# A four-layer graph network: norm, projections, split and logits of three graph stages, and one graph tail, each as one pipeline over node tiles

## The chip, the cores and the metric

The kernel runs on one core of a Trainium2 chip. The metric is the device time of one execution in microseconds; before the change it was 7021.22 us in the median of three runs (7018.96 to 7030.24). A core has a matmul engine (PE, with its weight loads as PEld), VectorE (DVE), ScalarE (ACT), GpSimd (POOL) and SyncE (SP), each with its own queue, and 16 DMA engines. They meet only through semaphores.

## The reference, cut to what matters

3125 nodes with 256 features, 53,125 edges. Each of four layers adds a graph stage, a mixing stage and a feed-forward stage to `x`. The change lies in the graph stages of layers 1 to 3.

```
xn = _layernorm(x)
# layer 1, graph stage
enh = xn + 0.1 * query_emb
Q, K, V = enh @ Wq + bq, enh @ Wk + bk, enh @ Wv + bv     # 4 heads of 64
scores  = sum(Q[dst] * (K[src] + 0.2 * rel)) / 8
agg     = segment_sum(softmax over dst(scores) * V[src], dst)
msgs    = where(deg > 0, agg, V)
y       = msgs @ Wo + bo + xn
g1      = (y - mean(y)) / sqrt(var(y) + 1e-5) * gamma + beta
x       = x + g1 + mix1(xn)
# layer 2: h = xn @ W + b; h_src = sum(h * a_src), h_trg = sum(h * a_trg), 8 heads of 32
# layer 3: support = xn @ weight; relu(segment_sum(support[src] * edge_weight, dst))
```

## The kernel before

The nodes are 25 tiles (`NT`) of 125 rows (`P`). `core.x`, `core.xn` hold them by rows, `core.xnT` by columns (the transposes of the normed rows). The program is a sequence of phases (`Phase`, line 81); each is a block with one program per engine, and closes with a barrier of all engines (line 97) that the trace names as `PEq L97` or `POOLq L97`. Within a phase the order on each engine is the order written, and waits are on semaphores. Nothing is scheduled by a planner.

Before each of the graph stages of layers 1 to 3 stands `layer_norm` (line 502): 25 statistics (line 546), thirteen small instructions over all tiles (552 to 565), then five tiles at a time the normed rows (595), two transposes a tile (651), the copy to `xnT` (637) and in layers 1 and 3 the copy to `xn` (614). `project` (line 655) loads its weights, multiplies 25 tiles (714) and adds the bias on the way out of PSUM (740, 745) or copies (757); with a `table` it writes five tiles per DMA through a ring of two slots (695).

Layer 1 (`gnn1`, line 3457): norm; `g1_enh` adds the query embedding to `xnT`; `project` for the queries; `split_rows` (2835) cuts them into three bf16 parts, in turns of ScalarE and VectorE; `project` for keys and values into the table `keyval1`; then `edge_scores` gathers rows of that table (3169). After scores and softmax `weighted_sums` (3373) reads weighted rows (`kept`) back, scales them on GpSimd (3414), sums them by node on the matmul engine (3425) and adds them up on VectorE (3439) in 440 steps. The tail: `g1_fin` reads all values back (3504) and chooses between sum and own value (3515 to 3521) in whole-tensor instructions, `transpose_rows` (2798), `project` with `Wo`, `add_rows` (3537), and `layer_norm` with gamma, beta and the addition to `x` (573 to 582).

Layer 2 (`gnn2_mix2`, line 3775): norm, `project`, then `g2_logit` with the two logit sums over all tiles (3809, 3810) and the table write (3799, 3802), and the addition of another bias to `x`. Then comes `linear_attention`, whose weights are loaded at lines 967 to 973. Layer 3 (`gnn3_mix3`, line 2570): norm, `project` into the table `support`, then the mixing stage, which gathers from it (837).

## Time and profile before

| | |
|---|---|
| median of three runs | 7021.22 us (7018.96 to 7030.24) |
| the profiled execution's own time | 7018.5 us |
| its span | 7016.7 us |
| mean granted matmul clock | 0.758 of full |
| PE busy | 4600.0 us (66%) |
| DVE busy | 3445.3 us (49%) |
| POOL busy | 2631.8 us (38%) |
| ACT busy | 1006.0 us (14%) |
| DMA | 616.64 MB, mean 88 GB/s |

The shares are means over stages with different limits: no engine is busy throughout, and the stretches that the change touches are read one by one below. Times in the rows are microseconds from the span's start unless marked ns.

### The profile page before, as it was taken

What the parts mean: (1) busy time and instruction counts of PE and PEld (TensorE: products, weight loads), DVE (VectorE), ACT (ScalarE), POOL (GpSimd) and SP (SyncE); (2) the same over time, 40 slices, a digit from 0 to 9 for tenths busy, and PEclk for the clock granted to TensorE, in tenths of its full rate; (3) what the DMA queues carried; (4) which work ended last, traced back from release to release, by engine and by line L of the source; (5) the groups of instructions that cost most, each with busy time, mean ns of one, the idle gap of its engine ahead of it and who ended that gap; (6) DMA issues with size and microseconds to landing.
All of it is one profiled execution on the core that took longest, in us unless ns stands there. A gap on an engine that the chain in (4) does not pass through costs nothing. (4 is left out here: it accounts for less than half of the span.)

```text
span 7016.7 us, 71368 instructions
## 1 busy us (share of the span) xinstructions
PE 4600.0 (66%) x17936; PEld 3173.8 (45%) x17936; DVE 3445.3 (49%) x8060; ACT 1006.0 (14%) x2236; POOL 2631.8 (38%) x2698
## 2 busy tenths in 40 slices
PE   0486755556784577748736646588759986767644
PEld 0244543334572343324335533476637764545443
DVE  6224444443004567769851255577742233566722
ACT  0121100002221000001112210000023331111111
POOL 2345556661100455537512200566500004555332
PEclk9877776667896575559858877656679998888767
DMA  4100013333111788856512210344410003222223
GB/s 141 46 2 2 2 40 92 92 92 82 37 39 43 224 254 255 249 166 197 153 64 82 78 36 0 100 114 114 94 38 0 0 0 104 71 73 72 68 91 108
DMA packets 407468, 616.64 MB, mean 88 GB/s; under 512 B 76191, under 2 KB 303918, under 8 KB 406741
## 3 DMA queue, kind: packets, MB, share of 16 engines
q0 software_dynamic: 124448, 324.61, 16.9%
q1 hardware_dynamic: 279540, 284.98, 12.9%
q10 hardware_dynamic: 3154, 3.20, 0.2%
q8 instruction: 144, 2.36, 0.1%
q14 instruction: 182, 1.48, 0.1%
HBM read 475.70 MB, written 137.50 MB: 87 GB/s over the span
## 5 line engine op out<-in xcount | busy, mean ns | idle before, releaser
L837 POOL DMA_INDIRECT m_rows<-support,far_at x440 | 421.7, 958 | 1133.1 <-POOLq L97 775.5
L3169 POOL DMA_INDIRECT g_sc_rows<-keyval,src_at x440 | 438.6, 997 | 520.0 <-DVE g1b_scores L3239 227.6
L3576 POOL DMA_INDIRECT g_sp_rows<-h,src_at x440 | 438.0, 996 | 464.6 <-POOLq L97 254.1
L493 POOL DMA_INDIRECT records<-record,place_at x416 | 416.2, 1001 | 408.5 <-issue 114.4
L847 PE MATMUL g_sums_bank<-g_sums_rows,g_sums_same 128*125 128x256 f32 x880 | 351.0, 536 | 292.6 <-issue 279.2
L837 POOL DMA_INDIRECT g_sums_rows<-h,far_at x440 | 416.0, 945 | 230.1 <-issue 111.1
L3624 PE MATMUL g_sp_bank<-g_sp_rows,g_sp_same 128*125 128x264 f32 x880 | 456.7, 618 | 46.0 <-issue 22.7
L3188 PE MATMUL g_sc_pair<-g1q_parts,g_sc_near 125*128 x1320 | 333.0, 384 | 170.8 <-DVE g_sc_rows L3235 112.0
L847 PEld LDWEIGHTS g_sums_bank<-g_sums_rows,g_sums_same 128*125 128x125 f32 x880 | 197.8, 255 | 445.7 <-issue 397.7
L847 PE MATMUL m_half<-m_rows,m_same 128*125 128x256 f32 x880 | 292.3, 436 | 130.5 <-issue 125.6
L879 DVE TENSOR_TENSOR g_total<-g_total,g_sums_bank 125x256 f32 x440 | 182.8, 415 | 332.9 <-issue 158.5
L879 DVE TENSOR_TENSOR g_total<-g_total,m_half 125x256 f32 x440 | 183.2, 416 | 276.2 <-PE m_half L847 187.0
L3596 PEld LDWEIGHTS g_sp_near_bank<-g_both,g_sp_near 125*128 125x128 f32 x880 | 247.5, 294 | 149.1 <-issue 86.2
L3425 PE MATMUL g_sp_bank<-g_sp_rows,g_sp_same 128*125 128x260 f32 x880 | 281.8, 421 | 27.8 <-ACT g_sp_rows L3405 13.7
L3414 POOL TENSOR_TENSOR g_sp_rows<-g_sp_rows,g_alpha 128x512 f32<-128x512 f32 x220 | 227.3, 1043 | 148.8 <-DMA g_sp_rows<-kept 143.7
L1493 DVE SCALAR_TENSOR_TENSOR x<-f_y,f_comb,x 125x256 f32 x200 | 96.7, 484 | 377.9 <-PE f_y L1310 377.6
L847 PEld LDWEIGHTS m_half<-m_rows,m_same 128*125 128x125 f32 x880 | 159.1, 206 | 240.5 <-issue 174.8
L1695 POOL DMA_INDIRECT f_back<-answer_rows,f_place_at x100 | 94.8, 948 | 412.1 <-DMA answer_rows<-f_answer 382.2
L3231 DVE TENSOR_TENSOR g_sc_rows<-g_sc_rows,g_sc_pair 128x512 f32<-128x512 f32 x220 | 149.8, 681 | 198.5 <-PE g_sc_pair L3191 120.7
L3188 PEld LDWEIGHTS g_sc_pair<-g1q_parts,g_sc_near 125*128 125x128 bf16 x1320 | 137.2, 120 | 237.6 <-issue 188.9
L1352 ACT ACTIVATE f_hid<-f_h,f_shift,f_scale 128x375 f32<-128x375 f32 (+1 forms) x320 | 195.7, 612 | 287.6 <-PE f_h L1289 281.9
L3624 PEld LDWEIGHTS g_sp_bank<-g_sp_rows,g_sp_same 128*125 128x125 f32 x880 | 203.9, 286 | 57.0 <-issue 33.6
(663 smaller groups left out, 9749.0 us busy)
## 6 DMA issues: line engine op xcount, KB each, us to landing
kept<-g_sc_rows SPq DMA_DIRECT2D x440, 128.0 KB
g_sp_rows<-kept SPq DMA_DIRECT2D x440, 128.0 KB
xnT<-sorted_rows SPq DMA_DIRECT2D x80, 256.0 KB
answer_rows<-f_answer SPq DMA_DIRECT2D x64, 256.0 KB
g_sc_local_in<-local_rows SPq DMA_DIRECT2D x55, 250.0 KB
g_sp_local_in<-local_rows SPq DMA_DIRECT2D x55, 250.0 KB
answer_rows<-zero SPq DMA_DIRECT2D x1, 9856.0 KB
sorted_rows<-zero SPq DMA_DIRECT2D x1, 8192.0 KB
```

What stands on the lines that cost most here:

```text
L493: nc.gpsimd.indirect_dma_start(core.records, bass.IndirectOffsetOnAxis(ap=core.place_at[:, t:t + 1], axis=0), core.record[:, t, :], None). ...
L837: nc.gpsimd.indirect_dma_start(self.rows[:, k, :], None, self.table, bass.IndirectOffsetOnAxis(ap=core.far_at[:, s:s + 1], axis=0)).then_i ...
L847: nc.tensor.matmul(self.halves[s % slots], self.same[:, s % self.RING, :], self.rows[:, s % self.SLOTS, :], start=True, stop=True).then_in ...
L879: nc.vector.tensor_tensor(there, there, self.halves[s % len(self.halves)].unsqueeze(1), ALU.add).then_inc(self.added, 1)
L1352: nc.scalar.activation(hid[layer][:, i % 2, mo, 0:n], hbank[q % HR][:, 0:n], func, scale=scale[layer][:, g, mo:mo + 1], bias=shift[layer][ ...
L3169: nc.gpsimd.indirect_dma_start(rows[:, k, :], None, table, bass.IndirectOffsetOnAxis(ap=core.src_at[:, s:s + 1], axis=0)).then_inc(gathere ...
L3188: nc.tensor.matmul(banks[pair % PAIR_BANKS][:, s % 2, 0:D], near[:, g % 2, k * W:(k + 1) * W], query[:, i, bass.ds(tile, 1), :].rearrange( ...
L3414: nc.gpsimd.tensor_tensor(mine, mine, alpha[:, 2 * pair:2 * pair + 2, :].unsqueeze(3).to_broadcast([W, 2, heads, dim]), ALU.mult).then_inc ...
L3425: nc.tensor.matmul(banks[s % BANKS][0:P, 0:D + heads], same[:, s % RING, :], rows[:, s % SLOTS, :], start=True, stop=True).then_inc(summed, 1)
L3576: nc.gpsimd.indirect_dma_start(self.rows[:, k, :], None, self.table, bass.IndirectOffsetOnAxis(ap=core.src_at[:, s:s + 1], axis=0)).then_i ...
L3596: nc.tensor.matmul(self.near_banks[g % 2][:, k * heads:(k + 1) * heads], self.near[:, g % 2, k * W:(k + 1) * W], self.target[:, bass.ds(ti ...
L3624: nc.tensor.matmul(self.banks[s % self.BANKS][0:P, 0:D + self.heads], self.same[:, g % 2, k, :], self.rows[:, s % self.SLOTS, :], start=Tr ...
```

## The change

The norms, projections, the query split and the logits of the three graph stages become three functions, `gnn1_front`, `gnn2_front` and `gnn3_front`, and layer 1's tail becomes `gnn1_tail`; each is one phase in which all engines go through the tiles in turns. A helper, `NormTiles`, holds the norm: VectorE takes the statistics of five tiles while the five before them are in work, ScalarE writes the normed rows and copies the transposed columns. The query embedding is no longer added to every column but multiplied with the weights once and added to the biases; the logit vectors of layer 2 are folded into 16 further columns of its weights, and the addition of its other bias goes to GpSimd. The tables of layers 1 and 3 are written tile by tile through rings of 5 and 8 slots, that of layer 2 by five tiles. The values are read back, a tile at a time, in the weighted sums. In the tail the choice between sum and own value is a sum of two products with the identity in PSUM, and the statistics go in chunks of 4, 5, 5, 5 and 6 tiles. All loops are written out.

```diff
+class NormTiles:
...
+    def tile_stats(self, v, t):
+        nc, core = self.core.nc, self.core
+        nc.vector.bn_stats(self.halves[:, t, :], core.x[:, t, :]).then_inc(self.measured, 1)
...
+    def dve_turn(self, v, link, i):
+        o, k = divmod(i, BODY)
+        if o + 1 >= NODE_LOOPS:
+            return
+        first = (o + 1) * BODY
+        for t in (first, first + 1) if k == 0 else (first + k + 1,) if k + 1 < BODY else ():
+            self.tile_stats(v, t)
+        if k == BODY - 2:
+            self.spread(v, link, o + 1)
+        if k == BODY - 1:
+            self.refine(v, link, o + 1)
+
+    def act_turn(self, act, i):
+        nc, stat = self.core.nc, self.stat
+        if i < NT:
+            act.wait_ge(self.refined, i // BODY + 1)
+            nc.scalar.activation(self.out[:, i, :], self.core.x[:, i, :], ACT.Identity, scale=stat[:, 2, i:i + 1], bias=stat[:, 5, i:i + 1]).then_inc(self.normed, 1)
+        t = i - 1
+        if 0 <= t < NT:
+            act.wait_ge(self.turned, t + 1)
+            nc.scalar.activation(self.core.xnT[:, :, columns(t)], self.turns[t % 2][:, 0:DC * P].rearrange("p (c n) -> p c n", c=DC), ACT.Copy).then_inc(self.columns_kept, 1)
+        if i % BODY == BODY - 2 and i // BODY + 1 < NODE_LOOPS:
+            self.root(act, i // BODY + 1)
+
+    def turn(self, pe, t):
+        nc, core = self.core.nc, self.core
+        pe.wait_ge(self.normed, t + 1)
+        if t >= 2:
+            pe.wait_ge(self.columns_kept, t - 1)
+        for c in range(DC):
+            ins = nc.tensor.transpose(self.turns[t % 2][:, c * P:(c + 1) * P], self.out[:, t, c * 128:(c + 1) * 128], core.ident[0:P, 0:P])
+        ins.then_inc(self.turned, 1)
...
+def gnn3_front(core, table):
...
+    KEPT = 8
...
+            for t in range(NT):
+                sp.wait_ge(kept, t + 1)
+                sp.dma_start(nodes(table)[:, t, :], ring[:, t % KEPT, :]).then_inc(landed[t % KEPT], 16)
...
+                if s % GROUP == GROUP - 1 and s // GROUP < NT:
+                    t = s // GROUP
+                    sp.dma_start(own[:, t, :], nodes(values)[:, t, :]).then_inc(own_in, 16)
...
+def gnn1_front(core, table, parts):
...
+    KEPT, ROWS, LAG = 5, 6, 6
...
+            for i in range(NT + 1):
+                if i < NT:
+                    norm.turn(pe, i)
+                t = i - 1
+                if t < 0:
+                    continue
+                pe.wait_ge(norm.columns_kept, t + 1)
+                if t == 1:
+                    pe.wait_ge(bias_set, 2)
+                if t >= 2:
+                    pe.wait_ge(q_kept, t - 1)
+                for c in range(DC):
+                    ins = nc.tensor.matmul(qbank[t % 2][0:P, 0:D], core.xnT[:, c, columns(t)], w[:, c, 0:D], start=c == 0, stop=c == DC - 1)
+                ins.then_inc(q_made, 1)
+                if t >= 3:
+                    pe.wait_ge(kv_kept, t - 2)
+                for c in range(DC):
+                    ins = nc.tensor.matmul(kvbank[t % 3][0:P, :], core.xnT[:, c, columns(t)], w[:, c, D:3 * D], start=c == 0, stop=c == DC - 1)
+                ins.then_inc(kv_made, 1)
...
+            for i in range(NT + LAG):
+                norm.act_turn(act, i)
+                t = i - 3
+                if 0 <= t < NT:
+                    act.wait_ge(q_kept, t + 1)
+                    nc.scalar.activation(parts[:, 0, t, :], query[:, t % ROWS, :], ACT.Copy).then_inc(rounded[0], 1)
+                t = i - 5
+                if 0 <= t < NT:
+                    act.wait_ge(lessened[0], t + 1)
+                    nc.scalar.activation(parts[:, 1, t, :], query[:, t % ROWS, :], ACT.Copy).then_inc(rounded[1], 1)
+
+        @block.vector
+        def _(v):
+            link = Chain(v, chain_sem).link
+            for t in range(BODY):
+                norm.tile_stats(v, t)
+            norm.spread(v, link, 0)
+            v.wait_ge(loaded, 16 * 7)
+            link(nc.vector.tensor_scalar(emb[:], emb[:], 0.1, None, ALU.mult))
+            for c in range(DC):
+                nc.vector.tensor_scalar(embT[:, c, :], core.zero[:, 0:P], emb[:, c:c + 1], None, ALU.add).then_inc(spread_set, 1)
+            norm.refine(v, link, 0)
+            v.wait_ge(biased, 1)
+            nc.vector.tensor_tensor(b[:, 0:D], b[:, 0:D], qbank[1][0:P, 0:D], ALU.add).then_inc(bias_set, 1)
+            nc.vector.tensor_tensor(b[:, D:3 * D], b[:, D:3 * D], kvbank[2][0:P, :], ALU.add).then_inc(bias_set, 1)
+            v.wait_ge(bias_set, 2)
+            for i in range(NT + LAG):
+                norm.dve_turn(v, link, i)
+                t = i - 2
+                if 0 <= t < NT:
+                    v.wait_ge(q_made, t + 1)
+                    if t >= ROWS:
+                        v.wait_ge(lessened[1], t - ROWS + 1)
+                    nc.vector.tensor_tensor(query[:, t % ROWS, :], qbank[t % 2][0:P, 0:D], b[:, 0:D], ALU.add).then_inc(q_kept, 1)
+                    v.wait_ge(kv_made, t + 1)
+                    if t >= KEPT:
+                        v.wait_ge(landed[t % KEPT], 16 * (t // KEPT))
+                    nc.vector.tensor_tensor(ring[:, t % KEPT, :], kvbank[t % 3][0:P, :], b[:, D:3 * D], ALU.add).then_inc(kv_kept, 1)
+                t = i - 4
+                if 0 <= t < NT:
+                    v.wait_ge(rounded[0], t + 1)
+                    nc.vector.tensor_tensor(query[:, t % ROWS, :], query[:, t % ROWS, :], parts[:, 0, t, :], ALU.subtract).then_inc(lessened[0], 1)
+                t = i - 6
+                if 0 <= t < NT:
+                    v.wait_ge(rounded[1], t + 1)
+                    nc.vector.tensor_tensor(parts[:, 2, t, :], query[:, t % ROWS, :], parts[:, 1, t, :], ALU.subtract).then_inc(lessened[1], 1)
...
+def gnn1_tail(core, own, total, heads):
...
+    dim, RING = D // heads, 4
+    FIRST = [0, 4, 9, 14, 19, 25]
...
+            for i in range(NT + 14):
+                t = i
+                if t < NT:
+                    if t >= RING:
+                        pool.wait_ge(turned, t - RING + 1)
+                    nc.gpsimd.tensor_tensor(hd(alone[:, t % RING, :]), hd(own[:, t, :]), bcast_last(some[:, t, :], [P, heads, dim]), ALU.mult).then_inc(held, 1)
+                    if t == 0:
+                        pool.wait_ge(loaded, 16 * 4)
+                    nc.gpsimd.tensor_tensor(core.xn[:, t, :], core.xn[:, t, :], b[:], ALU.add).then_inc(rested, 1)
+                t = i - 14
+                if 0 <= t < NT:
+                    pool.wait_ge(normed, t + 1)
+                    nc.gpsimd.tensor_tensor(own[:, t, :], own[:, t, :], gamma[:], ALU.mult).then_inc(stretched, 1)
...
+                    for c in range(DC):
+                        there, mine = turns[i % 2][:, c * P:(c + 1) * P], slice(c * 128, (c + 1) * 128)
+                        nc.tensor.matmul(there, part[:, i % RING, mine], core.ident[0:P, 0:P], start=True, stop=False)
+                        ins = nc.tensor.matmul(there, alone[:, i % RING, mine], core.ident[0:P, 0:P], start=False, stop=True)
+                    ins.then_inc(turned, 1)
...
+                    for h in range(heads):
+                        nc.scalar.activation(part[:, t % RING, h * dim:(h + 1) * dim], total[:, t, h * dim:(h + 1) * dim], ACT.Copy,
+                                             scale=den[:, t, h:h + 1]).then_inc(scaled, 1)
...
+                t = i - 12
+                if 0 <= t < NT:
+                    act.wait_ge(refined, max(o for o in range(len(FIRST) - 1) if FIRST[o] <= t) + 1)
+                    nc.scalar.activation(own[:, t, :], own[:, t, :], ACT.Identity, scale=stat[:, 2, t:t + 1], bias=stat[:, 5, t:t + 1]).then_inc(normed, 1)
...
+                t = i - 3
+                if 0 <= t < NT:
+                    v.wait_ge(out_made, t + 1)
+                    v.wait_ge(rested, t + 1)
+                    nc.vector.tensor_tensor(own[:, t, :], outs[t % 3][0:P, 0:D], core.xn[:, t, :], ALU.add).then_inc(plussed, 1)
+                t = i - 4
+                if 0 <= t < NT:
+                    v.wait_ge(plussed, t + 1)
+                    nc.vector.bn_stats(halves[:, t, :], own[:, t, :]).then_inc(weighed, 1)
...
+                t = i - 4
+                if 0 <= t < NT:
+                    nc.vector.tensor_tensor(core.x[:, t, :], core.x[:, t, :], beta[:], ALU.add).then_inc(shared, 1)
+                t = i - 16
+                if 0 <= t < NT:
+                    v.wait_ge(stretched, t + 1)
+                    v.wait_ge(shared, t + 1)
+                    nc.vector.tensor_tensor(core.x[:, t, :], core.x[:, t, :], own[:, t, :], ALU.add).then_inc(finished, 1)
...
+def gnn2_front(core, table, hprime, both, own, saved, heads):
...
+            for o in range(NODE_LOOPS):
+                sp.wait_ge(h_kept, (o + 1) * BODY)
+                mine = slice(o * BODY, (o + 1) * BODY)
+                sp.dma_start(nodes(table[:, 0:D])[:, mine, :], hprime[:, mine, :]).then_inc(saved, 16)
+            sp.wait_ge(logit_kept, NT)
+            sp.dma_start(nodes(table[:, D:D + heads]), both[:, 0]).then_inc(saved, 16)
+            sp.wait_ge(loaded, 16 * 5)
...
+            v.wait_ge(loaded, 16 * 5)
+            for i in range(2):
+                link(nc.vector.tensor_tensor(prod[:, :, i, :], w[:, :, 0:D], bcast_mid(av[:, i, :], [128, DC, D]), ALU.mult))
+            for c in range(DC):
+                ins = nc.vector.tensor_reduce(w[:, c, D:full], prod[:, c].rearrange("p i (h d) -> p (i h) d", h=heads), AX.X, ALU.add)
+                ins.then_inc(folded, 1)
+            v.wait_ge(folded, 2)
...
+                    nc.vector.tensor_tensor(hprime[:, t, :], banks[t % 3][0:P, 0:D], b[:, 0:D], ALU.add).then_inc(h_kept, 1)
+                    nc.vector.tensor_tensor(both[:, :, t, :], banks[t % 3][0:P, D:full].rearrange("p (i h) -> p i h", i=2),
+                                            b[:, D:full].rearrange("p (i h) -> p i h", i=2), ALU.add).then_inc(logit_kept, 1)
...
-        project(core, "proj3", core.xnT, [("L3_gnn_weight", D)], None, D, table=table)
+        gnn3_front(core, table)
...
-        project(core, "g2_h", core.xnT, [("L2_gnn_W", D)], hprime, D, bias=[("L2_gnn_b", D)])
...
+        gnn2_front(core, table, hprime, both, own, saved, heads)
...
+                gnn1_front(core, table, parts)
...
+        weighted_sums(core, "g1_sp", kept, alpha, heads, total, own, values)
+        gnn1_tail(core, own, total, heads)
```

The matmul engine at the start of layer 1, before: transposes (`ln_bank`) in a loop over five tiles, then all query products, then all key and value products, in three phases.

```order
L651 MATMUL ln_bank<-ident,ln_tile 128x125 x2
L646 REGISTER_ALU
L646 COMPARE_AND_BRANCH
L100 UNCONDITIONAL_BRANCH
L714 MATMUL g_q_bank<-g_q_w,g1a_enhT 125x256 x50
L714 MATMUL g_kv_bank<-g_kv_w,g1a_enhT 125x512 x50
```

The same place of the change: first the products with the embedding, then the tiles (`xw` holds the normed rows).

```order
L3583 MATMUL g_front_q<-g_front_w,g_front_embT 125x256 x2
L3585 MATMUL g_front_kv<-g_front_w,g_front_embT 125x512 x2
L1710 MATMUL g_front_turn<-ident,xw 128x125 x4
L3599 MATMUL g_front_q<-g_front_w,xnT 125x256 x2
L3604 MATMUL g_front_kv<-g_front_w,xnT 125x512 x2
L1710 MATMUL g_front_turn<-ident,xw 128x125 x2
```

The transposes of tile t + 1 now stand ahead of the products of tile t, and the last three rows repeat for each tile.

VectorE in layer 1's tail, before: whole tensors of 6400 columns, and the statistics of all tiles behind each other.

```order
L3518 TENSOR_TENSOR g_total<-g_total,g_fin_den 125x25x256
L3520 TENSOR_TENSOR g_mid<-g_mid,g_fin_some 125x6400
L3521 TENSOR_TENSOR g_mid<-g_mid,g_total 125x6400
L745 TENSOR_TENSOR g_mid<-g_out_bank,g_out_b 125x256
L3537 TENSOR_TENSOR g_mid<-g_mid,xw 125x6400
L546 BN_STATS g_ln_halves<-g_mid 125x6
L577 TENSOR_TENSOR g_mid<-g_mid,g_ln_gamma 125x6400
L578 TENSOR_TENSOR g_mid<-g_mid,g_ln_beta 125x6400
L582 TENSOR_TENSOR x<-x,g_mid 125x6400
```

VectorE in the tail of the change, where the first chunk's statistics are closed (`g_own` holds the own values, later the result; the small instructions work on 4 columns).

```order
L3777 TENSOR_TENSOR g_own<-g_tail_out,xw 125x256
L3781 BN_STATS g_tail_halves<-g_own 125x6
L3789 TENSOR_TENSOR g_tail_stat<-g_tail_halves 125x4
L3790 TENSOR_TENSOR g_tail_stat<-g_tail_halves 125x4
L3791 TENSOR_TENSOR g_tail_stat<-g_tail_halves 125x4
L3792 TENSOR_SCALAR g_tail_stat<-g_tail_stat 125x4
L3793 TENSOR_TENSOR g_tail_stat<-g_tail_stat 125x4
L3794 TENSOR_SCALAR g_tail_stat<-g_tail_stat 125x4
L3795 SCALAR_TENSOR_TENSOR g_tail_stat<-g_tail_stat 125x4
L3796 RECIPROCAL g_tail_stat<-g_tail_stat 125x4
L3810 TENSOR_TENSOR x<-x,g_tail_beta 125x256
L3777 TENSOR_TENSOR g_own<-g_tail_out,xw 125x256
```

The small instructions now stand between the additions that free the product banks.

## Rows read from the trace of the kernel before

**Rows 1.** Time line, DVE and POOL: start, us, engine, line, operation [idle before].

```profile
2126.77 0.43 DVE L546 BATCH_NORM_STATS2 ln_halves<-x  x1 [2.96 <-PEq L97]
...
2297.15 0.95 POOL L3169 DMA_INDIRECT g_sc_rows<-keyval,src_at  x1 [176.00 <-POOLq L97]
```

**Rows 2.** Windows: us, busy PE, PEld, DVE, ACT, POOL, then PEclk, DMA share, GB/s.

```profile
2126.30:2163.00 36.70, 14.12 (x50) 7.30 (x50) 27.41 (x87) 11.03 (x27) 0.00 (x0) 0.50 0.00 0
...
2199.00:2224.00 25.00, 0.00 (x0) 0.00 (x0) 14.55 (x10) 18.60 (x15) 0.00 (x0) 0.57 0.00 0
2224.00:2297.00 73.00, 46.01 (x100) 19.71 (x100) 16.54 (x25) 0.00 (x0) 0.00 (x0) 0.80 0.26 99
```

**Rows 3.** Time line, DVE, then windows: the writing of table keyval.

```profile
2265.28 2.48 DVE L740 TENSOR_TENSOR g_kv_ring<-g_kv_bank,g_kv_b 125x512 f32<-125x512 f32 x4 [4.56 <-DMA keyval<-g_kv_ring]
...
2275.29 3.08 DVE L740 TENSOR_TENSOR g_kv_ring<-g_kv_bank,g_kv_b 125x512 f32<-125x512 f32 x5 [5.99 <-DMA keyval<-g_kv_ring]
...
2255.30:2275.30 20.00, 20.00 (x48) 8.62 (x47) 6.52 (x11) 0.00 (x0) 0.00 (x0) 1.00 0.33 129
...
2285.00:2295.30 10.30, 0.00 (x0) 0.00 (x0) 0.00 (x0) 0.00 (x0) 0.00 (x0) 0.50 0.31 122
```

**Rows 4.** Time line, DVE: layer 1's tail, from its beginning to the next stage.

```profile
3472.06 0.43 DVE L3439 TENSOR_TENSOR g_total<-g_total,g_sp_bank 125x260 f32 x1 [0.21 <-DVE g_total L3439]
...
3503.62 6.83 DVE L3520 TENSOR_TENSOR g_mid<-g_mid,g_fin_some 125x6400 f32<-125x6400 f32 x1 [22.00 <-DMA g_mid<-keyval]
...
3564.80 6.83 DVE L3537 TENSOR_TENSOR g_mid<-g_mid,xw 125x6400 f32<-125x6400 f32 x1 [1.11 <-PEq L97]
...
3614.56 1.73 DVE L1602 BATCH_NORM_STATS2 f_halves<-x 125x6 f32<-125x256 f32 x5 [1.77 <-PEq L97]
```

**Rows 5.** Time lines and a window: layer 2's front and the attention's start.

```profile
4054.25 8.26 DVE L546 BATCH_NORM_STATS2 ln_halves<-x  x25 [7.14 <-PEq L97]
...
4064.43 0.18 DVE L563 TENSOR_TENSOR ln_stat<-ln_stat 125x25 f32<-125x25 f32 x1
4064.65 0.18 DVE L564 TENSOR_SCALAR ln_stat<-ln_stat 125x25 f32<-125x25 f32 x1
...
4148.00:4150.00 2.00, 0.00 (x0) 0.00 (x0) 2.00 (x1) 0.00 (x0) 0.00 (x0) 0.50 0.57 17
...
4153.41 0.40 SPq L967 DMA_DIRECT2D m_att_wk<-in_L_mix_Wkv  x1
...
4158.96 2.08 PE L986 MATMUL m_att_sums<-zero 125*128 125x257 f32 x4 [49.35 <-DMA m_att_wout<-in_L_mix_Wproj]
```

**Rows 6.** Time lines, DVE and POOL: layer 3's front.

```profile
5756.38 8.27 DVE L546 BATCH_NORM_STATS2 ln_halves<-x  x25 [1.24 <-PEq L97]
...
5831.96 0.94 POOL L837 DMA_INDIRECT m_rows<-support,far_at  x1 [775.45 <-POOLq L97]
```

**Rows 7.** Time line, DVE: key and value additions at the matmul engine's pace.

```profile
2241.14 0.69 DVE L740 TENSOR_TENSOR g_kv_ring<-g_kv_bank,g_kv_b 125x512 f32<-125x512 f32 x1 [1.02 <-PE g_kv_bank L714]
...
2242.86 0.69 DVE L740 TENSOR_TENSOR g_kv_ring<-g_kv_bank,g_kv_b 125x512 f32<-125x512 f32 x1 [1.02 <-PE g_kv_bank L714]
```

**Rows 8.** Groups of ACT by line and shape: count, busy us, mean ns, idle before.

```profile
L637 ACT ACTIVATE xnT<-ln_bank 128x250 f32 x100 | 38.1, 381 | 67.3 <-PE ln_bank L651 60.9 <-issue 3.7
L1782 ACT ACTIVATE xnT<-f_bank,f_bcol,f_gcol 128x256 f32<-128x256 f32 x64 | 32.6, 562 | 165.9 <-PE f_bank L1727 88.5 <-issue 77.4
...
L2987 ACT ACTIVATE g_sc_mkvrow<-g_sc_mbank,g_sc_minverse 125x128 f32<-125x128 f32 x25 | 9.2, 368 | 82.6 <-DVE g_sc_mkvrow L3063 57.8 <-issue 17.9 <-PE g_sc_mbank L2950 6.9
```

**Rows 9.** The weighted sums of layer 1: a group of POOL, and a window.

```profile
L3414 POOL TENSOR_TENSOR g_sp_rows<-g_sp_rows,g_alpha 128x512 f32<-128x512 f32 x220 | 227.3, 1043 | 148.8 <-DMA g_sp_rows<-kept 143.7
...
3300.00:3400.00 100.00, 94.70 (x296) 43.06 (x294) 95.34 (x296) 15.42 (x74) 76.57 (x74) 1.00 0.66 195
```

**Rows 10.** Windows: transposes alone, and layer 2's sums.

```profile
4066.00:4082.00 16.00, 12.75 (x50) 7.30 (x50) 10.07 (x25) 9.49 (x25) 0.00 (x0) 0.56 0.00 0
4600.00:4625.00 25.00, 24.27 (x76) 19.58 (x75) 19.98 (x47) 1.07 (x4) 18.37 (x18) 0.50 0.44 117
```

446 lines of the change are left out of this document (300 added, 146 removed).

## The prediction

> **What bounds the kernel now.** I read the time line of each engine first, where the four edited stretches begin and end, because one core runs everything and every phase closes with a barrier of all engines: a phase costs what its slowest engine costs, plus its fill, its drain and its weight loads. The layer 1 front lasts from the first statistics at 2126.77 us to the first gather at 2297.15 us, in which GpSimd sat idle for 176.00 us [rows 1]. The reader is to see in the windows that each of its phases keeps one engine at work and none keeps two: in the norm VectorE is busy 27.41 of 36.70 us and the matmul engine 14.12, in the split the matmul engine not at all, in the key and value projection the matmul engine 46.01 of 73.00 us [rows 2]. Behind that projection stands the table write: VectorE waits for landings, ten microseconds apart for 1250 KB each, the DMA engines together busy for 0.33 and at 129 GB/s [rows 3]. That is a write on about five of the sixteen engines, and it goes on to 2295 us when no engine computes any more [rows 3].
>
> The tail of layer 1 runs from 3472.06 to 3614.56 us; 22.00 us of it are a wait for the reading back of the values, and whole-tensor VectorE instructions of 6.83 us follow each other with no other engine at work [rows 4]. The layer 2 front runs from 4054.25 us to the attention's first matmul at 4158.96 [rows 5], layer 3's from 5756.38 to 5831.96 [rows 6]. The four stretches are 170.4, 142.1, 104.7 and 75.6 us, 493 us of 7016.7. Outside them nothing changes but 25 loads in the weighted sums. So the question is only how long each pipeline takes.
>
> **Prices of a tile.** A 512 wide projection of a tile comes every 1.72 us at the full clock, so the 256 wide one takes half, 0.86 [rows 7]. Two transposes: 14.12 us for 50 at the low clock, 0.56 a tile, and less at the full one; I take 0.46 [rows 2]. VectorE: statistics 8.27 us for 25, 0.33 each; an addition of 256 columns out of PSUM 0.42 alone, 0.35 in a row, of 512 columns 0.69; a linked small instruction starts 0.22 us after the one before it [rows 5, 7]; a pass over 6400 columns 6.83 [rows 4]. There are 13 per five tiles: 2.8 us. ScalarE: copying a turned tile 0.38 us; with a scale and a bias from columns 0.56; with a scale alone 0.37 for 128 columns [rows 8]. Successive ones overlap by about 0.08.
>
> **Layer 1 front.** Seven loads stand at the start. Three issued from 4153.41 let the matmul engine start at 4158.96, 5.5 us later [rows 5]; with 0.45 for each further issue seven need 7.4. The four bias products then run at the low clock, 2 x 0.86 + 2 x 1.72 = 5.2 us. A tile costs the matmul engine 0.46 + 0.86 + 1.72 = 3.04, VectorE 0.33 + 0.35 + 0.62 + 2 x 0.33 + 0.56 = 2.5, ScalarE about 1.6, the table write 256 KB at 129 GB/s 2.0. The matmul engine is last: 25 x 3.04 = 76. Its work runs ahead of nobody's by more than a turn, so I add no wait. After it come one addition, one write with its latency and the last splits, 5 us, and the barrier, 1.9. Sum 95.5 against 170.4: **-75**. Here the norm, the split and the additions lie beneath the matmuls; if that cover failed wholly, the time would be that of the two engines in a row, 3.0 + 2.5 a tile, 62 us more. The write is covered as well, 2.0 under 3.04; were small writes as slow as 3.5 us each, the front would lose 12.
>
> **Tail of layer 1.** The read back is moved into the weighted sums and 22 us of waiting go; next late is the load of four weights, 5.9 us after the barrier's 0.9. A tile costs ScalarE four scalings of a head (0.37 less 64 columns at 0.83 ns, 0.315 each), a copy 0.38 and a norm 0.56, together 2.2 by durations and 1.75 by starts; VectorE 0.35 + 3 x 0.33 + 0.56 = 1.9; GpSimd three operations at half of 1.043 us, 1.6 with their overhead [rows 9]; the matmul engine four plain products against the identity, 4 x 0.21, and 0.86: 1.7. Four engines lie this close, so I take 2.1 and not the largest alone: 52. Fill at the low clock 3, the drain of the last chunk (13 small ones, a root, six norms, gamma, the sum) 8, the barrier 1.7. Sum 71.5 against 142.1: **-70**. Bounds: 1.9 a tile (ScalarE by starts) to 2.7 (an engine more than its rows say), -75 to -55. GpSimd has no elementwise instruction of 256 columns with two tensors in the trace but a copy; from below its price is that of the 512 wide one's half, from above the whole, 3 x 1.04 = 3.1 a tile, +25; I take the half, since 128 x 512 is the nearest row.
> The Trainium skill (SBUF - State Buffer, "Who interferes with whom") says that a VectorE instruction with two SBUF inputs and a GpSimd instruction that reads SBUF shut each other out. By that rule two of VectorE's three additions block GpSimd's three, about 2.4 a tile and the tail +8; no row here shows it, since in the weighted sums VectorE reads PSUM.
>
> **Layer 2 front.** Five loads: 6.3 us; four VectorE instructions over 512 columns that fold the logit vectors into the weights, 2.8, for which the first product waits. Then a ring decides the pace and not one engine: norms of five tiles wait for their statistics, and those stand in VectorE's row behind additions that wait for products. From one chunk's first turn to the next: two turns of the matmul engine 2 x 1.37, two additions 0.6, one statistic 0.33, eight small ones 1.75, the additions again 0.6, five small ones 1.1, norm 0.56, wake up 0.3: 8.0, or 1.6 a tile, 40 us. With 2 for the cold start and 1.3 for the last additions the phase ends 52.5 us after its start. VectorE's passes over 6400 columns (four of 6.8) are gone. But the attention's weights are now issued right behind the last table chunk (5.9 us by [rows 3]'s rate) and the logits' 3125 rows of 32 bytes, which before ran at 17 GB/s mostly under VectorE's last pass [rows 5]. 1.3 + 5.5 + 7.5 for that queue: first matmul 67 after the start, against 104.7: **-38**. Without the queue it is -45, with both transfers wholly in front -33.
>
> **Layer 3 front.** First norm after 6 us, then the same ring without the logits: 2 x 1.32 + 0.42 + 0.33 + 1.75 + 0.42 + 1.1 + 0.56 + 0.3 = 7.5 per five tiles, 37.5 in all; cold start 3, last copy and landing 3.5, barrier 1.9: 52 against 75.6: **-24**.
>
> **Weighted sums.** VectorE is busy 95.34 of 100 us [rows 9], the loads run 24 slots ahead and GpSimd is the one that waits for them (148.8 us idle). 25 more loads of 125 KB on five engines add 1.3 us of their time to every eight steps of 5.1 us, which takes those from a share near 0.66 to 0.91. Still below one, so +1, bounded by 0 and 10.
>
> **The clock.** In stretches that hold only transposes the granted clock was mostly the low level, 0.56 with the matmul engine busy 12.75 of 16 us; in the weighted sums, busy 94.70 of 100, it was 1.00; and in layer 2's sums it was 0.50 with the engine busy nearly all the time [rows 9, 10]. Layer 1's front is like the second. In the fronts of layers 2 and 3 transposes are a third of the work, so it may swing: at the low level a tile costs 0.5 + 1.72 = 2.2 instead of 1.5 to 1.6, 16 us more in each front. I charge 4 for both.
> The Trainium skill (TensorE: Matmul & The Clock Gate, "Part 4: PE-mode transpose") says that transposes do not count as work for the clock. By it products fill only 0.86 of 1.5 us here, and the full clock would not last; the pure transpose stretch agrees (0.56).
>
> The sum: 75 + 70 + 38 + 24 = 207, less 1 and 4, is 202. Own time of the profiled execution 7018.5 - 202 = 6816.5; the median of the runs shown is 2.7 above it, so **6819 us**.
>
> **Rivals.**
> 1. The clock stays low in both short fronts (chance 0.2). For it: the transposes above, and layer 2's sums; against: the products are 1.72 of 2.2 us as soon as the clock is low, which pulls it up again. +34 - 4: 6849 us. If the tail's 1.7 also doubled to 3.4 a tile, +32: 6881.
> 2. The turns run in lock step: each engine waits for another in each turn, so a tile costs two engines in a row (0.09). For it: rings of two and three banks; against: each wait refers to the turn before or earlier. +62 in layer 1's front, some 25, 25 and 45 in the others: 6976 us.
> 3. Writes tile by tile are slower than large ones (0.03). If each took 3.5 us on the five engines, layer 1's front would lose 25 x 0.46 = 12 and layer 3's 25 x 2 = 50: 6881. For it: each pays an issue and a landing of its own; against: the pieces of a row stay as large, and five or eight are in flight.
> 4. Slower than before (0.02): the own-value loads push five DMA engines over a share of one in the weighted sums, and their 440 steps follow the loads. It must cost more than 202 us: a step 0.46 us longer, 1.10 for 0.64. That decides from a share of 0.66 + 1.3/5.1 > 1, so from 1.8 us per extra load; the row gives 1.3 for 125 KB at the measured rate, and only the first 200 steps have one. Even then it would be 200 x 0.22.
> That the change does not do what it says is excluded by the order of the rows: the matmul engine alternates within one phase.
>
> **How the numbers follow.** Forecast 0.66, rivals 0.2, 0.09, 0.03 and 0.02. The forecast's own range is 6800 to 6840 (tail -75 to -55, queue -45 to -33, GpSimd). To hold 8 in 10 it must take in the first rival up to the doubled tail in part: 6790 to 6865. This kernel's measurement tells 0.2%, 14 us, from no change; all but the last rival lie far beyond it: faster 0.97, same 0.01, slower 0.02.
>
> **What would show it.** Between the first statistics of layer 1's front and the first gather about 96 us, key and value additions 3.0 us apart; 71 us from the end of the weighted sums to the next statistics, with ScalarE the busiest; 67 and 52 us for the others, a pause of the matmul engine every fifth tile; the granted clock 1.00 in the first and mixed in the others; the weighted sums at 0.64 us a step. I am wrong if additions come at 5 us, if a write's landing is what they wait for, or if the step grows.

## The result, and the profile after

The changed kernel takes 6823.17 us (median of four, 6816.83 to 6830.35) against 7025.35 (7018.96 to 7030.24), a ratio of 0.971 with an interval of 0.970 to 0.973; 6819 was forecast. The profiled execution took 6824.11 us with a span of 6822.3. The four stretches are read from the time lines, between the same two instructions as in [rows 1, 4, 5, 6]; the tail is counted from the end of the last addition of the weighted sums.

| stretch | before | forecast | after |
|---|---|---|---|
| layer 1's front | 170.4 | 95.5 | 92.1 |
| layer 1's tail | 142.1 | 71.5 | 83.6 |
| layer 2's front | 104.7 | 67 | 67.6 |
| layer 3's front | 75.6 | 52 | 46.7 |
| everything else in the span | 6524.0 | 6525 | 6532.4 |

The stretches save 202.9 us, the forecast had 207 less 4 for the clock. The 8.4 us that the rest grew by lie mainly in stretches that the change doesn't touch: before layer 1's front (3.2) and between the fronts of layers 2 and 3 (4.8). In e1 to e4 below the rest is 6516 to 6547 us with the same code there, so one execution differs from another by as much.

Layer 1's front, time line: its first statistics, two additions to keys and values with one left out between them, the first gather behind it, and a window of 65 us (busy PE, PEld, DVE, ACT, POOL, then PEclk, DMA share, GB/s).

```profile
2130.00 1.73 DVE L1638 BATCH_NORM_STATS2 g_front_halves<-x 125x6 f32<-125x256 f32 x5 [2.96 <-PEq L97]
...
2204.72 0.69 DVE L3647 TENSOR_TENSOR g_front_ring<-g_front_kv,g_front_b 125x512 f32<-125x512 f32 x1 [1.10 <-PE g_front_kv L3604]
...
2210.31 0.69 DVE L3647 TENSOR_TENSOR g_front_ring<-g_front_kv,g_front_b 125x512 f32<-125x512 f32 x1 [1.10 <-PE g_front_kv L3604]
...
2222.06 0.94 POOL L3252 DMA_INDIRECT g_sc_rows<-keyval,src_at  x1 [97.19 <-POOLq L97]
```

```profile
2150.00:2215.00 65.00, 65.00 (x231) 38.63 (x230) 50.40 (x155) 35.24 (x94) 0.00 (x0) 1.00 0.30 92
```

The matmul engine is busy 65.00 of 65.00 us at the full clock, where the windows of before showed one engine at a time [rows 2]. A tile comes every 2.80 us, and each addition waits for its product.

The tail. First the end of the weighted sums and the next stage's first statistics, then VectorE's row at one tile, and GpSimd beside it.

```profile
3397.16 0.43 DVE L3527 TENSOR_TENSOR g_total<-g_total,g_sp_bank 125x260 f32 x1 [0.21 <-DVE g_total L3527]
...
3440.49 0.80 DVE L3810 TENSOR_TENSOR x<-x,g_tail_beta 125x256 f32<-125x256 f32 x1
3441.21 0.83 DVE L3815 TENSOR_TENSOR x<-x,g_own 125x256 f32<-125x256 f32 x1
3441.97 0.41 DVE L3777 TENSOR_TENSOR g_own<-g_tail_out,xw 125x256 f32<-125x256 f32 x1
3442.30 0.41 DVE L3781 BATCH_NORM_STATS2 g_tail_halves<-g_own 125x6 f32<-125x256 f32 x1
...
3444.94 0.71 DVE L3789 TENSOR_TENSOR g_tail_stat<-g_tail_halves 125x5 f32<-125x5 f32 x1
...
3473.07 6.61 DVE L3815 TENSOR_TENSOR x<-x,g_own 125x256 f32<-125x256 f32 x10
3481.14 5.00 DVE L1602 BATCH_NORM_STATS2 f_halves<-x 125x6 f32<-125x256 f32 x15 [1.46 <-PEq L97]
```

```profile
3440.29 0.72 POOL L3710 TENSOR_TENSOR g_own<-g_own,g_tail_gamma 125x256 f32<-125x256 f32 x1 [0.94 <-ACT g_own L3762]
3440.97 0.80 POOL L3703 TENSOR_TENSOR g_tail_alone<-g_own,g_tail_some 125x256 f32<-125x256 f32 x1
3441.73 0.91 POOL L3706 TENSOR_TENSOR xw<-xw,g_tail_b 125x256 f32<-125x256 f32 x1
```

At this tile VectorE's additions of two SBUF tiles take twice what the one with an input in PSUM takes, and each ends some 0.28 us after a GpSimd instruction does. The statistics of a tile, with one SBUF input, are not lengthened beside GpSimd (0.41). A small instruction over five columns lasts 0.71 us; the same kind takes 0.17 in layer 3's front, where GpSimd computes nothing. Now the groups of the tail (count, busy us, mean ns, idle before).

```profile
L3710 POOL TENSOR_TENSOR g_own<-g_own,g_tail_gamma 125x256 f32<-125x256 f32 x25 | 19.4, 790 | 17.0 <-ACT g_own L3762 16.9
...
L3815 DVE TENSOR_TENSOR x<-x,g_own 125x256 f32<-125x256 f32 x25 | 15.4, 650 | 0.0
L3810 DVE TENSOR_TENSOR x<-x,g_tail_beta 125x256 f32<-125x256 f32 x25 | 14.6, 582 | 0.0
...
L3777 DVE TENSOR_TENSOR g_own<-g_tail_out,xw 125x256 f32<-125x256 f32 x25 | 10.4, 416 | 14.9 <-PE g_tail_out L3733 14.9
```

```profile
3415.00:3460.00 45.00, 37.87 (x252) 33.66 (x251) 41.84 (x111) 33.09 (x116) 33.99 (x49) 1.00 0.00 1
```

The window: VectorE, not ScalarE, is the busiest, 41.84 of 45 us.

Layers 2 and 3: the stretches' ends, the pauses of the matmul engine in layer 2, then the queue of SP (with the time that issuing took), and one window of each.

```profile
3921.78 1.73 DVE L1638 BATCH_NORM_STATS2 g_front_halves<-x 125x6 f32<-125x256 f32 x5 [6.87 <-PEq L97]
...
3947.25 0.43 PE L1710 MATMUL g_front_turn<-ident,xw 125*128 125x125 f32 x2 [1.02 <-ACT xw L1696]
...
3954.79 0.43 PE L1710 MATMUL g_front_turn<-ident,xw 125*128 125x125 f32 x2 [1.03 <-ACT xw L1696]
...
3989.39 2.08 PE L986 MATMUL m_att_sums<-zero 125*128 125x257 f32 x4 [18.49 <-DMA m_att_wout<-in_L_mix_Wproj]
...
5591.65 1.73 DVE L1638 BATCH_NORM_STATS2 g_front_halves<-x 125x6 f32<-125x256 f32 x5 [0.84 <-PEq L97]
...
5638.30 0.95 POOL L837 DMA_INDIRECT m_rows<-support,far_at  x1 [750.86 <-POOLq L97]
```

```profile
3971.69 2.21 SPq L4102 DMA_DIRECT2D h<-g_both  x1
3974.88 9.45 SPq L967 DMA_DIRECT2D m_att_wk<-in_L_mix_Wkv  x1
...
5600.77 31.65 SPq L2683 DMA_DIRECT2D support<-g_front_ring  x25
```

```profile
3945.00:3950.00 5.00, 3.76 (x19) 2.48 (x18) 4.62 (x22) 2.71 (x8) 1.77 (x3) 1.00 0.34 109
...
5625.00:5630.00 5.00, 5.00 (x29) 4.21 (x28) 1.93 (x5) 3.68 (x11) 0.00 (x0) 1.00 0.31 96
```

The pause comes every 7.54 us, every fifth tile, as forecast; the granted clock is 1.00 all the same. Behind the last product the attention waits 18.49 us for its weights, whose issue alone takes 9.45. In layer 3 the 25 writes leave in 31.65 us, 1.27 each, with a third of the DMA engines busy.

Layer 2's front also has GpSimd at work beside VectorE: it adds the mixing stage's bias to `x`. One small instruction in each chunk of five tiles waits for it.

```profile
3947.27 0.73 POOL L4110 TENSOR_TENSOR x<-x,g_front_bias 125x256 f32<-125x256 f32 x1 [2.52 <-ACT xw L1696]
3947.36 0.67 DVE L1668 TENSOR_TENSOR g_front_stat<-g_front_stat 125x5 f32<-125x5 f32 x1
...
5610.37 0.17 DVE L1668 TENSOR_TENSOR g_front_stat<-g_front_stat 125x5 f32<-125x5 f32 x1
```

The last row is the same instruction in layer 3's front.

### The profile page after: what moved, and what is told of

It is laid out like the page before. It is cut to its first block and busy times, and to the rows that moved or that the text cites. A ratio compares the mean times of both kernels' runs of the same rounds, so it can differ in the third digit from the quotient of the medians.

```text
span 6822.3 us, 70300 instructions
## 1 busy us (share of the span) xinstructions
PE 4616.8 (68%) x18094; PEld 3192.6 (47%) x18094; DVE 3394.2 (50%) x8258; ACT 1069.5 (16%) x2462; POOL 2708.0 (40%) x2773
```

## Experiments

Where "rest" is given it is the span less the four stretches. e1 to e4 ran on one chip, where the kernel before took 7031 us (one execution), e5 to e8 and e9 to e11 on two others, where it took 6622 and 6625. The four stretches of the changed kernel are the same on another chip within 0.7 us (e9), so stretches are compared across chips, and times only within one. The times of e7, e8, e9 and e11 are medians of four, the others single executions, from which only the stretches are used.

| run | front 1 | tail | front 2 | front 3 | rest | time | kernel before |
|---|---|---|---|---|---|---|---|
| e1 no GpSimd in the tail | 92.0 | 68.6 | 67.2 | 46.5 | 6532.6 | 6808.58 | 7030.89 |
| e2 beta early | 92.2 | 75.4 | 67.6 | 45.9 | 6547.0 | 6829.88 | 7030.89 |
| e3 statistics ahead | 91.8 | 82.7 | 66.4 | 46.0 | 6532.4 | 6821.10 | 7030.89 |
| e4 writes split | 92.0 | 83.1 | 59.5 | 44.4 | 6516.4 | 6797.17 | 7030.89 |
| e5 logits split | 92.3 | 83.8 | 63.6 | 46.5 | 6128.1 | 6416.11 | 6621.73 |
| e6 statistics further | 92.5 | 84.1 | 67.5 | 44.0 | 6117.2 | 6407.06 | 6621.73 |
| e7 tail as before | 92.6 | 142.6 | 67.5 | 46.4 | 6120.5 | 6474.88 | 6621.73 |
| e8 combined | 91.9 | 68.8 | 58.1 | 41.2 | 6116.3 | 6383.71 | 6621.73 |
| e9 changed again | 92.5 | 84.2 | 67.4 | 46.2 | 6136.9 | 6421.71 | 6625.27 |
| e10 GpSimd only writes | 92.1 | 68.5 | 67.3 | 46.2 | 6128.9 | 6404.76 | 6625.27 |
| e11 combined, second | 90.6 | 68.1 | 58.2 | 41.1 | 6129.8 | 6391.66 | 6625.27 |

**What lengthens the tail.** e1, GpSimd computes nothing there:

```diff
-  nc.gpsimd.tensor_tensor(hd(alone[..]), hd(own[..]), some, ALU.mult)   # and + b, and * gamma, with their waits
-  nc.tensor.matmul(there, alone[:, i % RING, mine], ...)
+  nc.tensor.matmul(there, own[:, i, mine], ...)
```

> The changed kernel, but GpSimd computes nothing in the tail of layer 1: the mask on the own values, the addition of the output bias and the multiplication with gamma are left out, the matmul engine reads the own values as they are. In the changed kernel the tail takes 83.6 us (forecast 71.5), VectorE is busy nearly all of its second half, and its additions of two SBUF tiles take 650 and 582 ns, those with one input in PSUM 416; small instructions of 5 columns take up to 0.66 us, in the fronts 0.165. Theory A (VectorE and GpSimd shut each other out at SBUF): both additions fall to about 0.41 us, every small instruction to 0.165, and the tail is then bound by ScalarE and the matmul engine near 1.8 us a tile: 71 to 75 us, the kernel about 10 us faster than the changed one. Theory B (two SBUF inputs cost VectorE this much by themselves, or because of the matmul engine's and ScalarE's reading): the durations stay at 0.58 to 0.65 us and the tail at 80 us or more. Theory C (GpSimd's own three operations, 2.2 us a tile, set the pace): the tail gets shorter, but VectorE's durations don't change.

The same two additions in its tail, by group:

```profile
L3795 DVE TENSOR_TENSOR x<-x,g_tail_beta 125x256 f32<-125x256 f32 x25 | 10.1, 406 | 0.0
L3800 DVE TENSOR_TENSOR x<-x,g_own 125x256 f32<-125x256 f32 x25 | 9.7, 417 | 0.1
```

406 and 417 ns in place of 582 and 650, and every small one at most 191: theory A, against B and C. The tail fell by 15.0, to 68.6, below the 71 to 75 expected. From the first tile's first product to the last tile's it took 43.1 us where it had taken 50.7, 1.80 and 2.11 a tile; most of the rest came from the drain, 12.2 us behind the last product for 18.9. In the sum over the tail VectorE's two wide additions took 10.2 us less and its small instructions 10.8 us for 19.3. The 15 us are an upper bound for the exclusion: e1 also leaves out GpSimd's own time, which in the drain stands between a tile's norm and its last addition.

e10, the same instructions as memsets, which read nothing:

```diff
-  nc.gpsimd.tensor_tensor(own[:, t, :], own[:, t, :], gamma[:], ALU.mult).then_inc(stretched, 1)
+  nc.gpsimd.memset(idle[:, 1, t % 8, :], 0.0).then_inc(stretched, 1)   # the other two likewise
```

> The changed kernel, but each of GpSimd's three operations in layer 1's tail is a memset of 256 columns: as many instructions with the same waits, that write SBUF and read nothing (mask, bias and gamma are left out, the matmul engine reads the own values as they are). Theory A1 (VectorE waits only for a GpSimd instruction that reads): VectorE's additions of two SBUF tiles take 0.41 us, small ones 0.165, and the tail takes the 69 us that it took without GpSimd. Theory A2 (any GpSimd instruction in SBUF shuts VectorE out): the additions are longer by about half a memset each, 0.45 to 0.6 us, and the tail takes 72 to 80.

```profile
L3814 DVE TENSOR_TENSOR x<-x,g_tail_beta 125x256 f32<-125x256 f32 x25 | 10.1, 406 | 0.0
...
L3819 DVE TENSOR_TENSOR x<-x,g_own 125x256 f32<-125x256 f32 x25 | 10.0, 419 | 0.2
...
L3708 POOL MEMSET g_tail_idle<- 125x256 f32 x25 | 7.8, 313 | 7.0 <-DMA g_tail_beta<-in_L_gnn_beta 7.0
...
L3796 DVE TENSOR_SCALAR g_tail_stat<-g_tail_stat 125x5 f32<-125x5 f32 (+2 forms) x5 | 0.9, 186 | 0.2
```

A1: 75 memsets of 0.31 us leave the additions at 406 and 419 ns and the tail at 68.5. Only one small form, the instruction with one tensor and a number, grew a little in two of its three lines (186 and 192 ns for 170). So it isn't GpSimd's activity or its semaphores, but its reading; whether a GpSimd operation with one input does the same wasn't tried. The Trainium skill (SBUF - State Buffer, "Who interferes with whom") states this for VectorE instructions with two SBUF inputs; the runs agree.

e2, one of VectorE's additions moved to where GpSimd is idle:

```diff
+  # layer 1's front, GpSimd
+  nc.gpsimd.tensor_tensor(core.x[:, t, :], core.x[:, t, :], beta[:], ALU.add)
-  # tail, VectorE
-  nc.vector.tensor_tensor(core.x[:, t, :], core.x[:, t, :], beta[:], ALU.add)
```

> The changed kernel, but x + beta is computed by GpSimd in layer 1's front, where it is idle, and no longer by VectorE in the tail. Tail: one addition of VectorE's (0.58 us) goes from each tile, 25 x 0.58 = 14.6 us of an engine that is busy 59 of 77 us. If VectorE with its waits for GpSimd is the bound (theory A) the tail falls from 83.6 to about 75 (ScalarE's and the matmul engine's 1.8 a tile stop it); if GpSimd is the bound (C) it stays within 2 us of 83.6. Front: GpSimd gets 25 instructions of about 0.73 us. By theory A they meet VectorE's two subtractions of SBUF tiles, so these grow from 0.42 to 0.5 or more in the mean, and the additions out of PSUM (0.42 and 0.69) do not; the front stays at 92 us, for the matmul engine's 2.80 us a tile cover it (VectorE at most 2.3 + 0.7). By theory B nothing grows in the front. Kernel: A 6815 us, C 6823.

Its front, groups of GpSimd's new addition, a subtraction in SBUF, and an addition out of PSUM:

```profile
L3585 POOL TENSOR_TENSOR x<-x,g_front_beta 125x256 f32<-125x256 f32 x25 | 18.2, 729 | 64.6 <-ACT xw L1696 64.5
...
L3661 DVE TENSOR_TENSOR g_front_query<-g_front_query,g1q_parts 125x256 f32<-125x256 f32 x25 | 12.4, 495 | 0.0
...
L3653 DVE TENSOR_TENSOR g_front_query<-g_front_q,g_front_b 125x256 f32<-125x256 f32 x25 | 10.2, 408 | 0.0
```

The tail took 75.4 (expected 75), with GpSimd's three operations a tile still in it. That excludes C as the bound of the changed kernel. In the front the subtraction that meets GpSimd grew from 0.42 to 0.495 and the addition out of PSUM stayed; the other subtraction, which writes bf16, stayed at 0.415 against what I expected. The front held its 92.2 us. The time, 6829.88, doesn't show the gain, since the rest took 15 us more than in the runs beside it; the stretch does.

**What sets layers 2 and 3.** e3 and e6 move the statistics ahead (e6 shown):

```diff
-  for t in (first, first + 1) if k == 0 else (first + k + 1,) if k + 1 < BODY else ():
+  for t in ((first, first + 1, first + 2), (first + 3, first + 4), (), (), ())[k]:
-  if k == BODY - 2: self.spread(...)      # and root
+  if k == 1: self.spread(...)             # root at 3
-  if k == BODY - 1: self.refine(...)
+  if k == 3: self.refine(...)
```

> The changed kernel, but in the three fronts the statistics of the next five tiles are measured in the first three turns of a chunk, spread in the third and refined in the fourth, and no longer in the fourth and fifth. Layer 1's front is bound by the matmul engine (2.80 us a tile without a pause) and stays at 92 us. In layer 2's front the ring over norm, product, addition and statistics sets 7.55 us per five tiles, with a pause of the matmul engine of 1.0 + 0.2 us in each. If that ring is the bound, the pauses go, five tiles cost 5 x 1.13 = 5.65 us, the last product ends about 4 x 1.9 = 7.6 us earlier, and the first matmul of the attention 5 to 8 us earlier if the queue behind it moves along (67.6 to about 61); if the chunk writes (5 x 5.9 us of the DMA engines) have become the bound it gains under 3. In layer 3 the ring was 6.83 per five tiles, but a write of 125 KB leaves every 1.27 us, 6.35 per five: at most 2 us are gained, 46.7 to 45. Kernel 6814 to 6819 us. Should the pauses stay, the ring wasn't it.

> The changed kernel, with the statistics of the next five tiles further ahead than in the run before: all five in a chunk's first two turns, the eight small instructions in the second turn, root and refinement in the fourth. The earlier attempt moved the pause from 1.23 to 1.25 us and the ring from 7.55 to 7.23 us per five tiles, since ScalarE then waited in its row for the inverse before it normed the next tile. Ring theory: now ScalarE finds the inverse ready, the pause falls under 0.4 us and five tiles cost what VectorE's own row costs, 5 x 0.33 + 5 x 0.42 + 13 x 0.2 = 6.4 us: products end about 4 us sooner than with 7.55 and layer 2's front takes 63 to 65 (the queue behind it stays, 18 us); layer 3 stays within 1 us of 46, its writes leave at 6.35 us per five. Rival (the pause is the norm and turning of a new chunk in itself, wake-ups between four engines): the pause stays above 1 us wherever the statistics stand, 66 to 67 us.

In e3 the pause stayed (1.25 us), the ring went from 7.54 to 7.23 and front 2 gained 1.2: expected 5 to 8, a miss, because ScalarE had to take the root in its row before it could norm on. In e6 the wait for ScalarE is gone and another stands there:

```profile
3704.86 1.15 PE L4128 MATMUL g_front_h<-g_front_w,xnT 128*125 128x272 f32 x4 [0.84 <-DVE g_both L4156]
...
3711.95 1.15 PE L4128 MATMUL g_front_h<-g_front_w,xnT 128*125 128x272 f32 x4 [0.84 <-DVE g_both L4156]
```

Five tiles take 7.09 us, and the matmul engine waits for VectorE's additions: VectorE's row was nearly the whole ring, it costs about 7.1 and not the 6.4 that I had added up. Its rows show what the sum lacked, two small instructions that wait for GpSimd:

```profile
3705.14 0.73 POOL L4110 TENSOR_TENSOR x<-x,g_front_bias 125x256 f32<-125x256 f32 x1 [1.66 <-ACT xw L1696]
3705.23 0.66 DVE L1666 TENSOR_TENSOR g_front_stat<-g_front_stat 125x5 f32<-125x5 f32 x1
...
3710.00 0.59 DVE L1649 TENSOR_SCALAR g_front_stat<-g_front_stat 125x5 f32<-125x5 f32 x1
```

At 0.17 each they would give 0.9 us back. Front 2 gained nothing (63 to 65 expected, a miss): the last product came 1.7 us sooner and the wait behind it grew from 18.5 to 20.2. Layer 3's front gained 2.4. So in layer 2 the end is set by the transfers.

e4 and e5 change these alone:

```diff
-  sp.dma_start(nodes(table[:, D:D + heads]), both[:, 0]).then_inc(saved, 16)
+  for p in (slice(0, 112), slice(112, P)):
+      sp.dma_start(nodes(table[:, D:D + heads])[p], both[p, 0]).then_inc(saved, 16)
   # e5: the logits only; e4: also the chunks of h and the tiles of support
```

> The changed kernel, but every table write of layers 2 and 3 is two transfers, partitions 0 to 111 and 112 to 124, in place of one of 125 partitions (layer 1's writes stay). In the trace transfers of 125 partitions keep a share of 0.31 to 0.34 of the sixteen DMA engines busy, five of them, at 98 to 109 GB/s. Theory W (five engines, since 125 divides by five only; 112 divides by sixteen): the share rises to over 0.6 while such a write runs, a write of 112 KB takes a third of the time, layer 3's front ends with the last copy and a landing of some 2 us, not 5.6 us later: 46.7 to 43; in layer 2 the last chunk and the logits pass faster, the issue of the attention's first weights takes less than its 9.45 us, and the first matmul comes at 57 to 61 after the start, not 67.6. Theory I (the queue's issuing is the limit, 3125 rows of 32 bytes at 3 ns each): the issue still takes 9 us, and layer 2's front stays within 2 us of 67.6. Kernel: W 6810, I 6821.

> The changed kernel, but of layer 2's table writes only the logits' one is split into partitions 0 to 111 and 112 to 124; the five chunk writes of 1250 KB stay whole. With all writes split the front took 59.5 us instead of 67.6, the issue of the attention's first weights 0.41 us instead of 9.45, and from the end of the last product to the attention's first matmul it was 10.9 us instead of 18.5. If the 3125 rows of 32 bytes on five engines (625 each, against 195 when sixteen and thirteen share them) are what holds the queue, this alone gives most of it: issue under 2 us, 12 to 14 us behind the last product, front 61 to 63. If the last chunk's five-engine write holds it, the front stays at 66 to 68 and only the issue gets shorter.

e4, time lines of SP's queue and of the matmul engine, then a window behind the last chunk:

```profile
3958.51 3.49 SPq L4105 DMA_DIRECT2D h<-g_both  x2
3962.97 0.41 SPq L967 DMA_DIRECT2D m_att_wk<-in_L_mix_Wkv  x1
...
3968.05 2.08 PE L986 MATMUL m_att_sums<-zero 125*128 125x257 f32 x4 [10.90 <-DMA m_att_wout<-in_L_mix_Wproj]
```

```profile
3960.00:3965.00 5.00, 0.00 (x0) 0.00 (x0) 0.00 (x0) 0.00 (x0) 0.11 (x1) 0.60 0.63 92
```

W: the share of DMA engines is 0.63 in a window over the logits and the start of the weights, and from 3959 to 3961 us, with the last chunk under way, 0.99 at 247 GB/s, where the changed kernel had 0.34 at 105 (3971 to 3974 us). The issue of the weights takes 0.41 us for 9.45, the wait behind the last product is 10.9 for 18.5, front 2 took 59.5 (57 to 61 expected), front 3 44.4 (43 expected). Part of the time in issuing only moved ahead, to the two transfers of the logits: with them it was 3.9 us for 11.7. e5 gives half of the gain, 63.6 (61 to 63 expected), with 14.6 us behind the last product, and there the logits' two issues took 7.75 us: the logits' small rows and the last chunk both count. That five engines serve 125 partitions is what the shares of 0.31 to 0.34 say; the Trainium skill (DMA: Bandwidth & Descriptors, "Why a DMA increments its semaphore by 16 and not by 1") gives the rule, the largest divisor up to sixteen, and e4 agrees.

**Whether the terms add.** e7 puts the tail and the weighted sums back as they were:

```diff
-  weighted_sums(core, "g1_sp", kept, alpha, heads, total, own, values)
-  gnn1_tail(core, own, total, heads)
+  weighted_sums(core, "g1_sp", kept, alpha, heads, total)
+  ...                                      # g1_fin, transpose_rows, project, add_rows, layer_norm
```

> The changed kernel with layer 1's tail and weighted sums as they were before: the values read back at the tail's start, four passes over whole tensors, turning, projection, residual and norm as phases of their own. If the terms add up as the stretches of the two traces say, the tail takes 142 us again instead of 83.6 and the kernel 6824 + 58.5 = 6882 us, 0.980 of the kernel before (forecast by the prediction's term of 70: 6893, 0.982). If the 25 loads of own values slow the weighted sums (rival 4, bounded by 10 us), their 292.8 us get shorter by that here; I expect no more than 1 us of it, so 292 to 293.

The tail took 142.6 again. Ratio 0.978 (0.977 to 0.980): 146.9 us below the kernel before, and the three fronts' stretches say 144.3. The weighted sums, from their first product to their last addition, take 300.8 us without the 25 loads, 300.7 with them in the changed kernel: rival 4 has nothing.

e9 is the changed kernel again, beside e11 on one chip.

> The changed kernel itself once more, beside the kernel before and the combined version on one chip, since two chips gave the kernel before 7031 and 6622 us. Stretches of the four edits as in the first trace within 0.7 us each (92.1, 83.6, 67.6, 46.7); what differs between chips lies outside them, in the stretches of gathers. On a chip of the slower kind ratio 0.971, on one of the faster kind (202 to 205 us of 6622) 0.969 to 0.970.

Ratio 0.970 (0.968 to 0.971), 203.6 us of 6625; the stretches lie within 0.7 us of the first trace, as expected.

**A version with all of it.** e8 joins e2, e4 and e6, adds the output bias by GpSimd during the weighted sums and loads the tail's weights there; e11 also splits layer 1's table write and gives gamma's last five products to VectorE:

```diff
+  # weighted sums, GpSimd, every fourth pair
+  nc.gpsimd.tensor_tensor(core.xn[:, t, :], core.xn[:, t, :], b[:], ALU.add).then_inc(rested, 1)
+  # weighted sums, SP, once: b, w, gamma
+  # e11, tail, VectorE, t >= 20
+  link(nc.vector.tensor_tensor(own[:, t, :], own[:, t, :], gamma[:], ALU.mult))
```

> All edits that the earlier runs speak for, together in the changed kernel, nothing left out: table writes of layers 2 and 3 split into 112 and 13 partitions; statistics of the fronts further ahead; beta added by GpSimd in layer 1's front; the output bias added by GpSimd in the weighted sums, where it is idle for 23 of 100 us and VectorE reads only one SBUF tile; the tail's weights loaded during the weighted sums. Tail: the loads' 6.9 us at its start go, VectorE's beta addition and one of GpSimd's three operations (0.77 us) go, ScalarE and the matmul engine are left at 1.8 us a tile: 1.3 + 3 + 25 x 1.8 + 8 + 1.5 = 59 us against 83.6 (theory A: GpSimd blocks VectorE for 1.45 instead of 2.2 us a tile; by C no less than 25 x 1.45 + 13, also reached). Layer 2: 59.5 less 3 = 56. Layer 3: 44 to 42. Weighted sums: 292.8, if 25 additions of 0.73 us on GpSimd stay in its gaps; up to 10 more if they don't. Sum against the changed kernel 25 + 11 + 4 = 40: 6783 us, 0.9655 of the kernel before. Rival: GpSimd falls behind in the weighted sums and the matmul engine waits for its products, +5 to +15 there.

> The combined version with two more edits: layer 1's table write split into 112 and 13 partitions as well, and the multiplication with gamma for the last five tiles of the tail on VectorE in place of GpSimd (0.33 + 0.2 + 0.33 us a tile instead of 0.66 + waits for GpSimd's 0.73, which shut each other out). The drain of the tail (5 tiles) gets 1 to 2 us shorter, 68.8 to 67.5, and the front of layer 1 up to 2 us (the last write of 250 KB lands sooner), 92 to 90.5. Beside the changed kernel: 15 + 9.5 + 5.5 + 3 = 33 us faster, 0.995 of it. If the 13-partition transfers cost issue time that the front's queue doesn't have, layer 1's front stays at 92.

e8: 0.964 (0.963 to 0.966) of the kernel before, e11: 0.965 (0.963 to 0.967), beside the changed kernel's 0.970 on e11's chip; 6391.66 against 6421.71 is 30 us (33 expected), half a percent, with no overlap between the four executions of each. The weighted sums stayed (300.3), front 2 came to 58.1 (56 expected) and front 3 to 41.2 (42 to 44 expected); the tail to 68.8 where I expected 59. The pace was the one expected, 1.84 us a tile; the miss lies in the fill, 7.0 us to the first product for 4.3, and in the drain, 16.6 for 9.5. Without GpSimd the drain was 12.2 (e1), so it was sized too short even so, and GpSimd adds to it. VectorE and GpSimd in e8's tail:

```profile
3179.86 0.72 POOL L3719 TENSOR_TENSOR g_own<-g_own,g_gamma 125x256 f32<-125x256 f32 x1 [0.46 <-ACT g_own L3770]
3179.87 0.74 DVE L3800 TENSOR_TENSOR g_tail_stat<-g_tail_stat 125x5 f32<-125x5 f32 x1
...
3180.54 0.61 POOL L3715 TENSOR_TENSOR g_tail_alone<-g_own,g_tail_some 125x256 f32<-125x256 f32 x1
...
3180.64 0.54 DVE L3801 TENSOR_SCALAR g_tail_stat<-g_tail_stat 125x5 f32<-125x5 f32 x1
...
3211.60 6.61 DVE L3818 TENSOR_TENSOR x<-x,g_own 125x256 f32<-125x256 f32 x10
```

A VectorE instruction over five columns waits out a whole GpSimd operation, twice in a row, and in the drain the ten last additions take 6.61 us as before. e11's two edits gave 0.7 and 1.3 us in their stretches, against e8 on another chip, where a stretch repeats within 0.7; e8 and e11 can't be told apart by time.

## Why the prediction was right, and where not

The total lies 4 us from the forecast, and partly by luck: the tail took 12.1 us more than its term, the fronts of layers 1 and 3 took 8.7 less, the charges for the clock and the weighted sums (5) weren't needed, and the rest of the profiled execution was 8.4 longer than before.

**Layer 1's front (-75, measured -78.3).** The matmul engine as the one bound, everything else beneath it: right. The term 3.04 a tile was 2.80, since two transposes between products cost 0.22 us (2148.56 to 2148.78 on its time line), not 0.46; the start took 15.0 instead of 12.6, mostly since the seven loads needed 9.2 for 7.4.

**Tail (-70, measured -58.5).** The wrong size, by 12.1 us: 9.2 of it in the drain, 3.1 in the fill (12.9 for 9.8). The 2.1 us a tile were measured (2.11), but for another reason: with GpSimd silent the pace is 1.80 (e1), and VectorE, which waits for GpSimd's reads, made it 2.11. The drain was sized at 9.7 us with the barrier and took 18.9: VectorE was behind when the last product came (its last addition out of PSUM ended 4.9 us later, 2.2 in e1), and of the ten last additions most alternated with GpSimd's last gammas, 6.61 us. Even without GpSimd it took 12.2. The sentence on the exclusion in the prediction put it at +8; with it the tail would have been forecast at 79.5, and the exclusion cost at most 15 (e1). That sentence counted only wide additions, two of VectorE's three; many of the thirteen small instructions of a chunk wait as well. GpSimd's price, half of 1.04, was 0.62 to 0.73 in the median, inside the bounds and not itself the pace (e2 ran at 1.97 us a tile with the same three operations).

**Layer 2's front (-38, measured -37.1).** Right in sum by two errors: 7.54 for 8.0 us per five tiles, so that the last product came 49.1 us after the start for 51.2, and behind it 18.5 us for the 15.6 of last additions and queue. The queue's terms can't be redone from the rows that the prediction names: 640 KB at the 129 GB/s of [rows 3] are 5.0 us and not 5.9, and the logits' 100 KB at 17 GB/s are 5.9, where the sum has 7.5. That the queue counts was right (e4); that the ring counts beside it was not: e6 shortened the ring and gained nothing. Only with the writes split did moving the statistics bring 1.4 us (e8 against e4).

**Layer 3's front (-24, measured -28.9).** The ring of 7.5 measured 6.84, the first norm came after 4.6 instead of 6 us. Of what is left, 2.3 us are five-engine writes (e4).

**Weighted sums (+1): 0** (e7). **Clock (+4): 0.** It rose in the first turns of every front and then stayed at 1.00 to the last products, transposes or not, so rival 1 is out: with products for 0.92 of the 1.13 us from one tile to the next (0.22 for its two transposes) the full clock held, and the pauses didn't lower it. The Trainium skill (TensorE: Matmul & The Clock Gate, "Part 4: PE-mode transpose") says that transposes don't count as work for the clock; what the prediction made of it, that the full clock would not last, didn't come true. Whether transposes count no run here shows, since none takes them out. Lock step (rival 2) and slow writes (rival 3) are out by the 2.80 and the 1.27 us.

## What to carry to other kernels

Where phases each use one engine, a pipeline over tiles costs its slowest engine per tile; but read, for each pair of VectorE and GpSimd that will now run side by side, where their inputs lie. Where GpSimd's instruction reads SBUF and VectorE's has two inputs there, add their times up, small instructions included, and put GpSimd's work where VectorE reads PSUM. In e8's and e6's rows a small instruction with one tensor and a number waited too. The end of such a phase is worth a line of its own: who is behind when the last product lands, and what stands in the DMA queue in front of the next phase's weights.

Here a transfer of 125 rows kept about five of the sixteen DMA engines busy (share 0.31 to 0.34); two transfers of 112 and 13 rows took 8 us out of one front (e4).

## What the runs showed that was not expected

Beside GpSimd's reads VectorE instructions of five columns last up to 0.74 us (e8), for 0.17, and not only those of two tensors: the form with one tensor and a number took 0.54. It also happens in layer 2's front, with which the prediction didn't reckon (0.67, and 0.66 and 0.59 in e6): moving its bias addition away from the small instructions is a change that wasn't tried.

The same kernel is 6% faster on another chip (7031 and 6622 us before the change). None of it lies in the four stretches, the weighted sums (300.7 and 300.8 us) or the feed-forward stage behind them (440.6 and 439.4); 96 us of the some 400 lie in the edge scores, which gather. A window of 100 us of the edge scores, the changed kernel on the first chip, then e7 on the other:

```profile
2300.00:2400.00 100.00, 76.10 (x439) 43.89 (x439) 66.27 (x127) 0.00 (x0) 56.35 (x58) 0.61 0.83 252
```

```profile
2200.00:2300.00 100.00, 85.94 (x542) 51.97 (x540) 79.49 (x152) 10.51 (x37) 67.21 (x71) 0.76 0.95 312
```

71 gathers issued for 58, 312 GB/s for 252, both windows in the first third of the stage; near its end the two are closer (268 and 253 GB/s). From the first gather to the weighted sums' first product it was 874.8 us and 778.4. Why the gathers are faster there wasn't tried. A change that saves a fixed number of microseconds has another ratio there, and only stretches can be compared.
